# A graph kernel's last pass, worked in quads of 512 nodes in place of pairs of 256

## The reference

```
def layer(h, W, b):                       # called three times
    h = h @ W.T
    msg = h[src] * norm[:, None]          # norm = dinv[src] * dinv[dst]
    agg = segment_sum(msg, dst, n)        # self loops included
    return relu(agg + b)
...
x = _layernorm(x + _L1_gnn_ref(...), axis=-1)   # (x - mean) / sqrt(var + 1e-5)
```

## Time and profile before

| | |
|---|---|
| three runs | 4437.53, 4458.02, 5122.97 us (median 4458.02) |
| profiled execution | 4450.03 us, its span 4448.3 us, mean granted clock 0.97 |
| HBM over the span | 651.69 MB read, 308.28 MB written, 216 GB/s |
| busy over the span | PE 90%, DVE 84%, ACT 60%, POOL 50% |
| last pass | from 3767.0 us, its first gather, to the end at 4448.3 us |

### The profile page before, as it was taken

The page is one execution under the profiler, slowest core; times in us unless marked ns, Lnnn a source line. Parts: engine busy times, 40 slices in busy tenths (PEclk is TensorE's granted clock), DMA queues, the critical chain, the costliest instruction groups (busy, mean ns, idle before and its releaser), DMA issues. The chain is left out here.

```text
span 4448.3 us, 107968 instructions
## 1 busy us (share of the span) xinstructions
PE 3981.7 (90%) x27934; PEld 3560.4 (80%) x27934; DVE 3717.4 (84%) x10652; ACT 2647.1 (60%) x6276; POOL 2234.4 (50%) x1972
## 2 busy tenths in 40 slices
PE   6559999999999997999978889887898887999999
PEld 1149999999999986888868888886888887888887
DVE  8737777777777768999968888886888886999999
ACT  0015555555555556888857877775787776344444
POOL 0044444444444410000057777767777775777776
PEclk9869999999999998999989999998999999999999
DMA  0154444444444428999966767665677766999998
GB/s 23 2 108 136 137 137 135 135 136 135 137 135 136 136 75 294 375 374 375 375 193 210 217 206 213 207 192 176 213 217 210 213 211 186 294 311 310 311 310 285
DMA packets 871189, 909.87 MB, mean 205 GB/s; under 512 B 154170, under 2 KB 770580, under 8 KB 871060
## 3 DMA queue, kind: packets, MB, share of 16 engines
q1 hardware_dynamic: 744400, 702.74, 48.3%
q0 software_dynamic: 94080, 205.13, 17.0%
q10 hardware_dynamic: 32580, 0.52, 0.4%
HBM read 651.69 MB, written 308.28 MB: 216 GB/s over the span
## 5 line engine op out<-in xcount | busy, mean ns | idle before, releaser
L460 POOL DMA_INDIRECT rows<-ga_scratch,node_i x980 | 1092.1, 1114 | 1005.8 <-POOLq L596 707.6
L460 POOL DMA_INDIRECT rows<-x_in,node_i x490 | 567.4, 1158 | 812.4 <-DVE raw L913 617.7
L460 POOL DMA_INDIRECT rows<-gb_scratch,node_i x490 | 571.6, 1167 | 181.5 <-issue 169.4
L488 PE MATMUL gcn_agg_ps<-gcn_rows_hi,gcn_select 128*128 128x256 f32 x2156 | 580.0, 304 | 33.6 <-DVE gcn_rows_lo L1258 33.6
L488 PE MATMUL gcn_agg_ps<-gcn_rows_lo,gcn_select 128*128 128x256 f32 x2156 | 546.9, 288 | 0.0
L860 ACT ACTIVATE h1t_hi<-h1t_ps,b_sb 128x256 fp32r<-128x256 f32 x392 | 164.3, 470 | 628.9 <-issue 493.6
L1378 PE MATMUL fin_agg_ps<-rows,fin_select 128*128 128x256 f32 x2156 | 530.9, 380 | 0.0
L1277 ACT CAST gcn_rows_hi<-rows 128x768 fp32r<-128x768 f32 (+1 forms) x392 | 286.3, 731 | 332.3 <-DMA rows<-gb_scratch,node_i 161.9
L1378 PEld LDWEIGHTS fin_agg_ps<-rows,fin_select 128*128 128x128 f32 x2156 | 411.0, 191 | 56.3
L488 PEld LDWEIGHTS gcn_agg_ps<-gcn_rows_hi,gcn_select 128*128 128x128 f32 x2156 | 421.9, 196 | 34.6 <-DVE gcn_rows_lo L1258 34.6
L515 PE MATMUL gcn_g_ps<-g_hi,gcn_ht_hi 128*128 128x256 f32 x1568 | 444.0, 283 | 0.7 <-ACT gcn_g L1296 0.7
(11 more groups left out here) (156 smaller groups left out, 12437.1 us busy)
## 6 DMA issues: line engine op xcount, KB each, us to landing
own<-x_in SPq DMA_DIRECT2D x196, 256.0 KB, 2.6
h_scratch<-h2t SPq DMA_DIRECT2D x196, 256.0 KB, 2.0
h2t_in<-h_scratch SPq DMA_DIRECT2D x196, 256.0 KB, 3.8
x_sb<-x_in SPq DMA_DIRECT2D x196, 256.0 KB, 4.8
x_scratch<-x SPq DMA_DIRECT2D x196, 256.0 KB, 4.9
ga_scratch<-g_out SPq DMA_DIRECT2D x196, 256.0 KB, 5.0
gcn_own<-ga_scratch SPq DMA_DIRECT2D x196, 256.0 KB
gb_scratch<-gcn_g SPq DMA_DIRECT2D x196, 256.0 KB, 3.4
```

The lines of the kernel that those rows point to most:

```text
L460: pool.indirect_dma_start(out=c["rows"][:, slot, b], out_offset=None, in_=source[:, :], in_offset=bass.IndirectOffsetOnAxis(ap=c["node"][: ...
L488: last = nc.tensor.matmul(out[:, j], select[:, b, j * P:(j + 1) * P], rows[:, pair.odd + b], start=n == 0, stop=n == len(terms) - 1)
```

## The change

The last pass is written anew on quads: every engine handles 512 nodes a step, with `quad_pipeline` (4 quads to a loop turn) in place of `pipeline`.

- SP: one load of 512 KB each of own and x1, and one store of 512 KB, for two of 256 KB each. The rings have 4 quads.
- PE: four identity matmuls ahead of the wait for the gathers, then the eleven with selections. PSUM has 2 buffers of a quad.
- DVE: the selection matrices are built by block, 5 instructions (256, 384, 384, 256 and 128 columns) for 7 of the same 1408 columns. `fin_h` has one buffer of a quad, `fin_res` two. `fin_res`, the reciprocal, `fin_shift` and the memset come once a quad; `fin_h` (4), statistics (4) and aggregates (4) stay one a tile. The selections now stand ahead of the statistics.
- ACT: `fin_sd` once a quad, `fin_y` still one a tile. Lags: PE 1; DVE 0, 2, 3; ACT 4 and, behind it, 2; store 5.
- POOL: the same gathers with the wait counted in quads.

The last pass's functions follow in the order PE, DVE, ACT; its last two pairs of lines are those of `fin_y` and of `fin_sd` on ACT.

```
+SPAN = [(0, 2), (0, 3), (1, 4), (2, 4), (3, 4)]
+def select_columns(nc, c, quad, select):
+    for b, (first, end) in enumerate(SPAN):
+        last = nc.vector.tensor_scalar(select[:, b, 0:(end - first) * P], c["iota32"][:, first * P:end * P],
+                                       c["place"][:, bass.ds(quad.q, 1), b], None, ALU.is_equal)
...
-        own = m.sb("fin_own", [P, RING, 2, D])
-        h = m.sb("fin_h", [P, 2, 2, D])
-        res = m.sb("fin_res", [P, RING, 2, D])
-        y = m.sb("fin_y", [P, RING, 2, D])
-        agg_ps = m.ps("fin_agg_ps", [P, 2, 2, D])
+        own = m.sb("fin_own", [P, QUAD_RING, 4, D])
+        h = m.sb("fin_h", [P, 4, D])
+        res = m.sb("fin_res", [P, 2, 4, D])
+        y = m.sb("fin_y", [P, QUAD_RING, 4, D])
+        agg_ps = m.ps("fin_agg_ps", [P, 2, 4, D])
...
-                    if pair := at(2):
+                    if quad := at(1):
...
+                        for j in range(4):
+                            nc.tensor.matmul(agg_ps[:, b, j], c["ident"][:], own[:, s, j], start=j % 2 == 0,
+                                             stop=False, skip_group_check=True)
+                        pe.wait_ge(gathered[s], quad.landed(BLOCKS))
+                        pe.wait_ge(select_done, quad.done())
...
-                    chosen, summed, scaled = at(0), at(3), at(5)
+                    chosen, summed, scaled = at(0), at(2), at(3)
...
-                        if pair.has(RING):
-                            dve.wait_ge(y_ready, pair.before(RING))
-                        nc.vector.scalar_tensor_tensor(out=res[:, s], in0=h[:, b], scalar=0.0, in1=x1[:, s],
+                        if quad.has(2):
+                            dve.wait_ge(y_ready, quad.before(2))
+                        nc.vector.scalar_tensor_tensor(out=res[:, b], in0=h[:], scalar=0.0, in1=x1[:, s],
...
+                        last.then_inc(stats_done, 1)
+                        dve.wait_ge(stats_done, quad.done())
...
+                        nc.vector.memset(c["spare"][:, 1:2], 0.0)
...
-                    if pair := at(6):
+                    if quad := at(4):
...
-                    if pair := at(4):
+                    if quad := at(2):
```

More of the change, by code:

```diff
@@ L448, in _, with __init__, done, before @@
                 nc.vector.tensor_scalar(c["place"][:], base[:], -1.0, None, ALU.add).then_inc(chain, 1)
-def gather_quads(nc, pool, c, source, gathered, rows_free):
+class Quad:
+    def __init__(self, group, place):
+        self.group, self.place = group, place
+        self.q = group * QUAD_RING + place
+        self.slot, self.turn, self.b = place, group, place % 2
+    def done(self, per=1):
+        return (self.q + 1) * per
+    def before(self, back):
+        return self.q + 1 - back
+    def has(self, back):
+        return not isinstance(self.q, int) or self.q >= back
+    def landed(self, dmas):
+        return (self.turn + 1) * (16 * dmas)
+    def tile(self, j):
+        return bass.ds(self.q * 4 + j, 1)
+def quad_pipeline(eng, step):
+    def group(number):
+        for k in range(QUAD_RING):
+            def quad_at(lag, k=k):
+                quad = Quad(number + (k - lag) // QUAD_RING, (k - lag) % QUAD_RING)
+                if isinstance(quad.q, int) and not 0 <= quad.q < NQ:
+                    return None
+                return quad
+            step(quad_at)
+    for number in range(QUAD_PEEL):
+        group(number)
+    with eng.Fori(QUAD_PEEL, NQ // QUAD_RING) as number:
+        group(number)
+    for number in range(NQ // QUAD_RING, -(-(NQ + QUAD_MAX_LAG) // QUAD_RING)):
+        group(number)
+def quad_rows(dram, q):
+    return dram[bass.ds(q * QUAD, QUAD), :].rearrange("(j p) d -> p j d", p=P)
+def load_quad(sp, fast, out, source, base, quad, landed, slot_free):
+    for ran, rows in ((1, source), (0, base)):
+        with sp.If(fast == ran):
+            if quad.has(QUAD_RING):
+                sp.wait_ge(slot_free, quad.before(QUAD_RING))
+            sp.dma_start(out, quad_rows(rows, quad.q)).then_inc(landed, 16)
+def gather_quads(nc, pool, c, source, gathered, rows_free, per):
     bound = pool.to_reg(NPAD - 1)
@@ L1388, in step @@
                 def step(at):
-                    chosen, summed, scaled = at(0), at(3), at(5)
[L1390 to L1393, removed]
+                    chosen, summed, scaled = at(0), at(2), at(3)
+                    if quad := summed:
+                        b = quad.b
+                        dve.wait_ge(agg_done, quad.done())
+                        if quad.has(1):
+                            dve.wait_ge(res_added, quad.before(1))
+                        for j in range(4):
@@ L1424, in step @@
[L1424 to L1430 removed]
+                            .then_inc(shift_ready, 1)
+                    if quad := chosen:
+                        if quad.has(2):
+                            dve.wait_ge(agg_done, quad.before(2))
+                        select_columns(nc, c, quad, select[:, quad.b]).then_inc(select_done, 1)
@@ L1432, in _ @@
+                quad_pipeline(dve, step)
             @block.scalar
```

153 lines of the change are left out of this document (74 added, 79 removed).

## The result

The changed kernel takes 4463.5 us (median of 7, 4450.13 to 4480.01) against 4449.31 (median of 7) for the kernel before; the ratio is 1.0039 with a 95% interval of 1.002 to 1.0058. One of the seven executions of the kernel before, at 5122.97 us, is a slow one and is left out of the ratio. The change costs 0.4%.

The account below looks back on a forecast made before the run. DVE and POOL both bound the last pass at about 6.7 us a quad. New quad 6.09 + 0.85 = 6.94; 3784.9 + 12.9 + 659.3 = 4457.1, then 13.3 and 1.7 give 4472 us, range 4440 to 4500.

Parts of the forecast that it names:

- DVE's work, 6.09: Last pass, DVE: its own instructions in the new quad sum to 6.09 us, against 6.757 a quad now.
- The closed chain, 6.94: DVE and ACT: `fin_res` waits for `fin_y` behind the root, idling DVE 0.85 us; the quad becomes 6.94 us.
- POOL at 6.7 gains on the rest until `agg_done` holds it: Last pass, gathers: POOL at 6.7 us a quad runs ahead of the 6.94 quad until held; nothing is lost.
- LOOP: Follow-up theory, not the prediction: the chain through ACT sets the quad; without `fin_res`'s wait it falls to 6.5 to 6.75.
- PE busy 93%: Middle stretches of the last pass: PE busy 93%, waiting 0.5 us a quad for the next selections.
- The ends: Start and finish of the last pass: first quad's sum at 3784.9, and 13.3 us from last `fin_h` to span's end.
- Even: Rival, last pass: DVE and POOL may wait for each other; chain at 6.76 or POOL at 6.72, 4454 us; chance 21%.
- Faster: Rival, last pass: DVE never waits for `fin_y`, POOL's bare 6.52 us a quad sets the pace, 4432 us; chance 7%.
- More collisions: Rival, DVE and POOL: selections and gather descriptors stretch each other, 7.2 us a quad for 4497, or 7.36 for some 4512; 9%.

Follow-up runs that it names:

- after: The changed kernel itself, as described under the change, set against the kernel before: 4463.5 us, ratio 1.0039.
- POOL's hold gone but the chain left: Changed kernel with `fin_h` written back into its PSUM buffer and read there by `fin_res`, ACT's order unchanged: 4460.12 us, one run.
- POOL out of the race: Changed kernel with four gathers a quad in place of five, the fifth block of edge rows left out: 4473.51 us, one run.
- the faster version: Changed kernel with ACT's outputs ahead of the root and `fin_h` written back into PSUM, where `fin_res` reads it: 4425.22 us, 0.9936 to the kernel before.
- iota in PSUM: Changed kernel with outputs ahead of the root, `fin_h` in PSUM, and selections comparing with an iota row in PSUM: 4458.49 us, 1.001.
- in halves: Changed kernel with outputs ahead of the root and `fin_res` as two instructions of 512 columns, operands in SBUF: 4749.24 us, one run on a slower chip.
- four buffers: Changed kernel with four buffers of a quad for `fin_res` in place of two, ACT's order unchanged: 4464.22 us, one run.

## Why the prediction was right

The time (4472, range 4440 to 4500; measured 4463.5) and the sign were right; it is 14 us over the kernel before by medians, where 14 over the median and 22 over the profiled execution were forecast. That the 14 agree to the microsecond is luck: the median of the kernel before was 4458 from three executions and is 4449 from seven. The last pass itself was forecast at 4470.4 - 3767.0 = 703.4 us and took 698.1, since a quad took 6.87 from the first `fin_h` to the last where 6.93 was worked out. By its steps:

- *DVE's work, 6.09.* From 4004.88 to 4011.45 are 6.57 us, less 0.47 of waiting: 6.10. `fin_res` took 1.15 for the 1.14 chosen (4007.09 to 4008.24), the selections 1.42 in place of 1.51, the statistics 1.43 for 1.46.
- *The closed chain, 6.94.* This is what sets the quad, 6.86 in after: DVE waits for `fin_y` and not for PE, and with POOL's hold gone but the chain left the quad is 6.87, with POOL out of the race 6.92. DVE's idle time is about 0.8 a quad, as 0.33 + 0.47 in the quad shown or 0.81 in one piece; forecast 0.85. The root starts 0.03 behind the aggregates and the outputs 0.21 behind the root.
- *POOL at 6.7 gains on the rest until `agg_done` holds it.* Wrong, and it is the step that failed. POOL's five steps took 6.88 us a quad from the first gather to the last, and it never waited for PE from 3800 to 4460 us. In 94 of 98 quads one step took 1.37 on average, since the cause is `fin_res`, whose 1024 columns hold it longer, and not the selections. The forecast had seen the 1.40 in the earlier trace rows beside the stretched selections in the earlier trace rows and put them together; the `fin_res` next to it was in the trace, but not among the rows shown. The error did not enter the sum, because PE's waits for gathers hardly reach DVE (0.6 us in the pass): POOL's 6.88 came out just under the chain, and that is luck. The same working would have given 6.5 to 6.75 for a kernel without the wait for `fin_y`, as LOOP did, and that one stands at 6.86. With the hold gone and the chain left, POOL waits 30.0 us in 500 for PE, so in after the hold seems to take up time in which POOL would have waited; this is argued and not shown.
- *PE busy 93%.* It was 96.13 us of 100. The forecast had a wait of 0.5 us for the selections in every quad; the waits show 22.5 us in 35 times on the weight loads, and 17.1 us in 24 times for gathers, which the forecast did not have.
- *The ends.* First `fin_h` 18.9 us behind the first gather (3799.03 against 3780.15) where 17.9 was worked out: the gather landed 1 us later, and the 11 matmuls took the 7.5 forecast. The end came 13.1 us behind the last `fin_h`, forecast 13.3.
- *The rivals.* "Even" needed the chain at 6.76; it is 6.86 or more. "Faster" (4432 at 6.52 a quad) is what the version with both limits gone does, 4425 at 6.52; the rival took only the chain away, which alone gives 6.86. "More collisions" named the right pair of engines and the wrong instruction. Its 0.42 us on POOL for one meeting, the length of a selection, was an estimate, and no run shows selections doing that. What the runs show is one hold a quad by `fin_res`: 94 steps of 1.37 us on average in after, each ending 0.87 us behind the end of `fin_res`. With one operand in PSUM 83 steps of the faster version began at least 0.05 us behind the start of a `fin_res` that still ran 0.14 us later, and they took 1.00 us on average. The selections cost POOL 0.1 to 0.2 us in 9 steps of 490 there, each ending 0.87 us behind the end of a selection with 384 columns. They cost VectorE more: 33 of its 196 selections with 384 columns took 0.48 to 0.64 us for 0.41, and all 33 end 0.16 us behind the end of a gather's step. With iota in PSUM all 196 take 0.60 to 0.61.

## What to carry to other kernels

When a change halves the number of instructions, look at what each buffer count now means in time: two buffers of a quad put the writer behind a chain that four of a pair had kept away, and turning two blocks of ScalarE's order takes it out. The lags show this ahead of any run. `fin_res` of pair n was worked in step n+3 and the outputs that it waited for, those of n-4, in step n+2, a whole step ahead; in quads both fall in step n+2. Here a `fin_res` with both operands in SBUF (0.69 us with 512 columns, 1.22 with 1024) held a gather's step that began at least 0.05 us behind its start until 0.87 us behind its end. With one operand in PSUM no step took over 1.21 us, and in halves none behind the first took over 1.47 where it had been 1.99; both are worth a try when GpSimd is near the bound. If two limits stand at the same height, taking away either shows nothing in the time: take away both in one run before calling a cause refuted.

## What the runs showed of the hardware

A step of an indirect gather on GpSimd, 128 rows of 1 KB, took 1.00 us (the mean of the 396 steps in after that no `fin_res` held). If `fin_res`, a `scalar_tensor_tensor` on VectorE with both operands in SBUF, had started at least 0.05 us before the step and still ran 0.14 us after the step's start, the step ended 0.87 us behind its end: 94 cases in after with a spread of 2 ns, 95 in the kernel before; the longest such step took 2.05 us (four buffers). A `fin_res` that started less than 0.03 us ahead of the step, or behind it, held nothing. It was hardly held itself: in after, 95 of 98 `fin_res` began inside a step and all took 1224 to 1227 ns, and the longest of 1024 columns in any run, 1283 ns with four buffers, began 0.03 us ahead of a step. With the first operand in PSUM the same instruction takes the same 1225 ns and no step exceeds 1.21 us. The other way round, a selection with its row in SBUF was longer beside a step: of 196 with 384 columns 61 took 0.52 to 0.58 us with four gathers, 33 took 0.48 to 0.64 in the faster version, and 94 took 0.45 to 0.46 in after, all ending 0.16 us behind a step. Without that, comparing 384 columns of an fp32 row in SBUF with a scalar took 0.41 us (431 ns over all in after), and 0.61 from PSUM.
